# Two layers of attention and feed-forward on one core: a DRAM store, an output transpose and a convolution wait are moved

## The chip, the cores and the metric

The kernel runs on one core of one Trainium2 chip. The metric is the device time of one launch in microseconds (us), the median of three runs. TensorE is PE in the rows (PEld is its weight load), VectorE is DVE, ScalarE is ACT, GpSimd is POOL, and SyncE is SP, which here issues DMAs.

## What is computed

Eight sequences of 512 tokens with 256 features go through two layers. Layer 0 is softmax attention with 16 heads plus a mixture of eight experts. Layer 1, where the change lies, is this (cut to what matters):

```python
def _L1_attn_ref(x, Wqkv_w, Wqkv_b, conv_w, conv_b, out_w, out_b):
    qkv = x @ Wqkv_w.T + Wqkv_b
    q, k, v = ...
    ctx = _causal_attn(q, k, v)
    ctx_c = ctx.reshape(b, s, d).transpose(0, 2, 1)
    conv_out = conv1d(ctx_c, conv_w, padding 1) + conv_b
    q2 = conv_out.transpose(0, 2, 1).reshape(b, s, NUM_HEADS, HEAD_DIM)
    ctx2 = _causal_attn(q2, k, v)
    return ctx2.reshape(b, s, d) @ out_w.T + out_b

xn = _layernorm(x, axis=-1)
x = x + _L1_attn_ref(xn, ...) + _L1_ffn_ref(xn, ...)
```

So each sequence has two causal attentions with the same keys and values: the second one's queries are the first one's output after a convolution over time of width three.

## The kernel before, in words

The kernel is written engine by engine. One class, Engine, holds the plan as generators that yield once per step; each engine's subclass fills in what it does at each step. All engines walk the same plan, so the plan fixes the order of the instructions on each of them, and semaphores (the waits `e.wait_ge`) tie them together. There is no scheduler.

A *unit* is one attention over 8 heads (half of a sequence's 16): `Unit(n, kind, b, c)` with b the sequence and c the half. Kind 0 is layer 0, kind 1 the first attention of layer 1, kind 2 the second. In layer 1 the order is two units of kind 1 (sequence b+1 or so), then two of kind 2 (sequence b), and so on, 32 units numbered 16 to 47. Each unit has two groups g of four heads.

`layer1` interleaves, in each of its rounds, five lanes, one step of each in turn:

- `expp`, the current unit: per step one bank of scores (`scores`, L1111, and the mask L1115), their exponential on ACT (L1959), and some steps later the product with V (`product`, L1128, into the bank PV). After the last product of a group, `close1` runs along with the following steps: `copy_o` (L1969, ACT copies PV to the tile O), `turn_o` (L1138, PE transposes O into bank Mb), `divide` (L1545 and L1553, DVE divides by the row sums and writes the context).
- `maxp`, the next unit: per step one bank of scores for the row maxima (`top`, PE L1072, DVE L1499). After a group, `shift` transposes the maxima (L1094), splits them into three bf16 parts on DVE (L1513 to L1521) and has SP write them as three extra rows of the queries (`rows`: three DMAs t_R<-t_msp of 4 KB). The next unit's scores of that group wait for them.
- `pre1`, the unit after the next: the projection (`part`, L1305 and L1311) for kind 1, or the transposes of the context (`turn_c`, L986) and the convolution (`convolve`, L1331) for kind 2; then the split of queries (z = 0) and keys (z = 1) into three bf16 parts: `high1` on ACT (L1943), `rest` on DVE (the residue t_rr, L1457), `low` on POOL (L2161, L2162), all into the tile spl. `fan1` on SP spreads the parts over the rows of QA or KA by six DMAs of 128 KB each (t_R<-t_spl). For kind 1, `values` on DVE writes V, and on SP it stores the key parts to DRAM (ks<-t_spl, 384 KB), from where the kind 2 unit of the same sequence fans them again (t_R<-ks).
- `fin1`, the unit before: for the second half of a kind 2 sequence the output projection: `turn_f` (L986), `keep_f` (ACT, L2079), `out` (L1354), `add_out`, `store`.
- a short lane in the first round.

Who shares what: bank Mb (`MB[1]`) is used by the query projection of kind 1, by turn_o, turn_c and turn_f; `mbank` waits until the earlier user has been read. The bank PV is free again after copy_o (`pv_read`). The tile cT is read by the convolution, and filled in two halves by ACT (`keep_c`, L2072, semaphore ct_done). All of SP's DMAs share one queue, in program order. On PE the instructions run in order; a wait holds back everything behind it.

Of the kernel before, what the change touches and what calls it, by code (L numbers as in the profile page):

```python
# [63 lines left out]
QK = {}  # L64
# [97 lines left out]
def steps(n):  # L162
    for _ in range(n):
        yield
# [373 lines left out]
class Engine:  # L538
# [216 lines left out]
    def maxp0(self, u):  # L755
        return steps(s1_uses(u))
# [112 lines left out]
    def values(self, u): pass  # L869
    def turn_c(self, u, c): pass  # L870
    def keep_c(self, u, c): pass
    def convolve(self, u, i): pass

    def fin1(self, u):

        if u.kind != 2 or u.c != 1:
            return
        yield from steps(7)
        for c in range(2):
            self.turn_f(u, c)  # L880
            yield
            self.keep_f(u, c)
            yield
        yield from steps(3)
        for h in range(2):
            self.out(u, h)
            yield
            self.add_out(u, h)
            yield
        self.store(u)  # L890
# [50 lines left out]
    def close1(self, u, g):  # L941

        yield
        self.copy_o(u, g)
        yield from steps(3)
        self.turn_o(u, g)
        yield
        self.divide(u, g)
        yield
# [20 lines left out]
class TensorE(Engine):  # L970
# [352 lines left out]
    def convolve(self, u, i):  # L1323
        e, m, s, b, c = self.e, self.m, self.s, u.b, u.c
        if i == 0:
            e.wait_ge(s.d_l2, 80)
            self.mbank(0, s.rr_done, QK[u.n, 0])
            e.wait_ge(s.pads, 1)
        k, cc = i // 2, i % 2
        e.wait_ge(s.ct_done, 2 * b + cc + 1)  # L1330
        t = self.nc.tensor.matmul(m.MB[0][:, :], m.CW[:, i, c * 128:c * 128 + 128], m.cT[:, cc, k:k + 512],  # L1331
                                  start=(i == 0), stop=(i == 5))
        if i == 5:
            t.then_inc(s.qk_mm, 1)
# [941 lines left out]
class SyncE(Engine):  # L2276
# [36 lines left out]
    def fan(self, u, z):  # L2313

        e, m, s = self.e, self.m, self.s
        if u.kind < 2 or z == 0:
            e.wait_ge(s.lo_done, QK[u.n, z])
            to, parts = ((m.QA[u.buf], QP), (m.KA[u.buf], KP))[z]
            of = [m.spl[:, z, p, :] for p in parts]
        else:  # L2320
            e.wait_ge(s.d_ks, 16 * (VN[1, u.b, u.c] - 16))
            to, of = m.KA[u.buf], [m.ks[2 * u.b + u.c][:, p, :].rearrange("(d h) n -> d h n", h=8) for p in KP]
        if u.n in (16, 17):
            e.wait_ge(s.ones_rows, 8)
        elif u.n == 18:
            e.wait_ge(s.y2_mm, 2 * NB)
        elif u.n >= 3:
            e.wait_ge(s.pv_mm, 8 * (u.n - 2))
        for j, part in enumerate(of):
            self.start(to[16 * j:16 * j + 16, :, :], part, s.d_f[z][u.buf])  # L2330

    def maxp0(self, u):
        for g in range(2):
# [57 lines left out]

    def fan1(self, u, z):
        self.fan(u, z)

    def values(self, u):

        self.e.wait_ge(self.s.lo_done, QK[u.n, 1])
        self.start(self.m.ks[2 * u.b + u.c], self.m.spl[:, 1, :, :], self.s.d_ks)

    def store(self, u):  # L2400
        e, m, s, b = self.e, self.m, self.s, u.b
# [101 lines left out]
```

## Time and profile before

| | |
|---|---|
| median of 3 runs | 1987.62 us (1987.46 to 2001.88) |
| profiled execution | 1987.46 us, of which the span from the first to the last instruction is 1985.3 us |
| PE busy | 1798.9 us (91% of the span) |
| DVE busy | 1253.8 us (63%) |
| ACT busy | 1023.6 us (52%) |
| POOL busy | 337.5 us (17%) |
| layer 1 | about 1145 to 1985 us |

Starts are us from the span's start. Busy times of PE overlap in part, since matmuls are pipelined and their ends are modelled. A wait is an engine's idle time with what ended it; idle time of PEld is no loss while PE still works. The distance of 2.16 us between the execution's time and the span lies around the first and last instruction.

### The profile page before, as it was taken

How to read it: one execution, taken by the hardware profiler on the slowest of the kernel's cores; microseconds unless marked ns; L12 is line 12 of the kernel's file. 1: busy time of each engine (PE TensorE's matmuls, PEld its weight loads, DVE VectorE, ACT ScalarE, POOL GpSimd, SP SyncE). 2: the span in 40 equal slices, each digit the busy share in tenths (PEclk: the TensorE clock that was granted, in tenths of full speed). 3: DMA queues.
4: the chain of work that ended last, by engine and by line, in shares of the span. 5: the costliest groups of instructions: out<-in, count | busy, mean ns of one | idle time of the engine just before them, and what ended most of it. 6: DMA issues, size and time to landing. Idle time of an engine off the chain costs nothing.

```text
span 1985.3 us, 31757 instructions
## 1 busy us (share of the span) xinstructions
PE 1798.9 (91%) x10745; PEld 878.4 (44%) x10745; DVE 1253.8 (63%) x3788; ACT 1023.6 (52%) x2064; POOL 337.5 (17%) x525
## 2 busy tenths in 40 slices
PE   4768999999889999998879898999999999999987
PEld 2313555555344454451234343455445454545444
DVE  6675555555654454457563776778787777787673
ACT  1444565555555555554644354555554555555454
POOL 2322211221111221123343200101010101111000
PEclk8878999999999999998999999999999999999999
DMA  6655333434654432441312363645454555455330
GB/s 158 179 143 124 74 68 81 78 76 89 158 125 65 73 59 44 64 57 33 93 33 43 49 83 54 82 74 71 73 72 75 69 84 74 74 84 74 60 50 22
DMA packets 144656, 155.80 MB, mean 78 GB/s; under 512 B 24697, under 2 KB 131473, under 8 KB 144497
## 3 DMA queue, kind: packets, MB, share of 16 engines
q1 hardware_dynamic: 123584, 114.71, 35.4%
q0 software_dynamic: 9024, 14.42, 4.1%
q10 hardware_dynamic: 11888, 24.64, 3.8%
q8 instruction: 87, 1.43, 0.3%
q14 instruction: 73, 0.59, 0.1%
HBM read 55.93 MB, written 33.69 MB: 45 GB/s over the span
## 4 chain that ended last, share of the span: by engine, by line
PE 65%; DVE 12%; DMA 9%; SPq 6%; issue 3%; ACT 2%; POOL 2%; ACTq 0%; DVEq 0%; POOLq 0%
PE p_PV L1128 11%; PE p_S L1111 9%; SPq L2297 6%; PE p_S L1072 5%; PE p_S L1055 5%; PE p_Ma L1331 4%; DMA t_R<-t_msp 4%; PE p_S L1188 4%; PE p_Ma L1211 4%; DVE p_S L1499 3%; PE p_S L1115 2%; DVE t_mx L1485 2%; PE p_Ma L1354 2%; DMA t_xTb<-xTd 1%; PE p_Mb L1211 1%
## 5 line engine op out<-in xcount | busy, mean ns | idle before, releaser
L1959 ACT ACTIVATE t_R<-p_S 128x512 f32<-128x512 f32 (+1 forms) x1216 | 682.7, 578 | 579.9 <-PE p_S L1115 396.1
L1499 DVE CUSTOM_DVE_ANT_0 p_S<-p_S,t_NM 128x128 f32<-128x128 f32 x1008 | 474.6, 514 | 200.3 <-PE p_S L1072 197.2
L1111 PE MATMUL p_S<-t_R 99*128 99x512 bf16 (+3 forms) x1536 | 477.7, 335 | 38.5 <-DMA t_R<-t_msp 17.0
L1485 DVE TENSOR_REDUCE t_mx<-p_S 128x1 f32<-128x512 f32 x512 | 347.0, 686 | 252.6 <-PE p_S L1055 250.5
L1128 PE MATMUL p_PV<-t_R 128*17 128x512 f32 (+3 forms) x3072 | 331.8, 504 | 1.3 <-ACT t_R L1959 1.0
L1072 PE MATMUL p_S<-t_R 96*128 96x128 bf16 x1008 | 254.5, 304 | 19.3 <-DMA t_R<-t_spl 10.2
L1111 PEld LDWEIGHTS p_S<-t_R 99*128 99x128 bf16 x1536 | 151.1, 99 | 179.0 <-ACT t_R L1959 69.0
L1055 PE MATMUL p_S<-t_R 96*128 96x512 bf16 x512 | 203.0, 399 | 27.0 <-DVE t_mx L1485 16.9
L1115 PE MATMUL p_S<-t_NM 128*128 128x128 bf16 x1024 | 199.2, 220 | 0.0
L2161 POOL CAST t_spl<-t_rr 128x512 bf16<-128x512 f32 x80 | 49.2, 615 | 866.8 <-DVE t_rr L1457 866.8
L1499 DVE DVE_READ_ACCUMULATOR2_ANT t_mx<- 128x1 f32 x1024 | 143.5, 140 | 0.1
L1072 PEld LDWEIGHTS p_S<-t_R 96*128 96x128 bf16 x1008 | 80.9, 98 | 139.6 <-DVE t_mx L1499 53.8
L1115 PEld LDWEIGHTS p_S<-t_NM 128*128 128x128 bf16 x1024 | 101.2, 99 | 68.7 <-issue 44.0
L1055 PEld LDWEIGHTS p_S<-t_R 96*128 96x128 bf16 x512 | 50.2, 99 | 168.7 <-issue 84.6
L1188 PE MATMUL p_S<-t_R,t_NM 128*128 x184 | 96.3, 605 | 6.8 <-DMA t_NM<-hTd 6.4
L1128 PEld LDWEIGHTS p_PV<-t_R 128*17 128x17 f32 x3072 | 51.1, 95 | 115.5 <-issue 112.9
L1331 PE MATMUL p_Ma<-t_NM,t_R 128*128 128x512 f32 x192 | 99.0, 612 | 0.1
L1211 PE MATMUL p_Ma<-t_R,t_NM 128*128 x360 | 94.6, 385 | 0.0
L2162 POOL TENSOR_TENSOR t_spl<-t_rr,t_spl 128x512 bf16<-128x512 f32 x80 | 93.2, 1164 | 6.5
L1211 PEld LDWEIGHTS p_Ma<-t_R,t_NM 128*128 128x128 f32 x360 | 68.2, 192 | 24.8 <-issue 10.2
L2046 ACT ACTIVATE t_R<-p_S,t_R 128x512 f32<-128x512 f32 x64 | 43.5, 687 | 61.3 <-PE p_S L1260 59.5
L2220 POOL DMA_DIRECT2D ysd<-t_NM x39 | 34.0, 871 | 215.1 <-ACT t_NM L2014 215.1
(282 smaller groups left out, 2153.7 us busy)
## 6 DMA issues: line engine op xcount, KB each, us to landing
t_R<-t_spl SPq DMA_DIRECT2D x480, 128.0 KB
t_R<-in_w ACTq DMA_DIRECT2D x32, 512.0 KB, 6.9
t_R<-ks SPq DMA_DIRECT2D x96, 128.0 KB
ks<-t_spl SPq DMA_DIRECT2D x16, 384.0 KB, 5.1
hTd<-t_NM SPq DMA_DIRECT2D x39, 128.0 KB, 2.6
ysd<-t_NM SPq DMA_DIRECT2D x39, 128.0 KB
t_NM<-hTd SPq DMA_DIRECT2D x39, 128.0 KB, 2.3
ysd<-t_NM POOLq DMA_DIRECT2D x39, 128.0 KB, 3.1
```

What stands on the lines that cost most here:

```text
L1055: self.nc.tensor.matmul(m.S1[s1_bank(k)][:, :], qa[0:96, 4 * g + j, qb * 128:(qb + 1) * 128], ka[0:96, 4 * g + j, 0:512], start=True, stop ...
L1072: t = self.nc.tensor.matmul(bank[:, z, :], qa[0:96, h, qb * 128:(qb + 1) * 128], ka[0:96, h, 0:n], start=True, stop=True)
L1111: t = self.nc.tensor.matmul(bank[:, z, :], ka[0:99, h, kb * 128:(kb + 1) * 128], qa[0:99, h, n0:512], start=True, stop=not u.causal)
L1115: t = self.nc.tensor.matmul(bank[:, z, 0:128], m.identb, m.maskk, start=False, stop=True)
L1128: t = self.nc.tensor.matmul(m.PV[32 * j:32 * j + 17, n0:512], vt[:, kb, 4 * g + j, :], m.P1[kb][j] if u.causal else m.P[p % 2][:, j, :], s ...
L1188: z = self.nc.tensor.matmul(m.MB[i][:, :], m.hT[t % 2][:, c, :], m.W1[:, bass.ds(self.regs[t], 1), c, :], start=(c == 0), stop=(c == 1))
L1211: x = self.nc.tensor.matmul(M[:, 0:256], m.AT[:, k, :], m.W2[:, bass.ds(self.regs[t], 1), k * 256:k * 256 + 256], start=(k == 0), stop=(p ...
L1331: t = self.nc.tensor.matmul(m.MB[0][:, :], m.CW[:, i, c * 128:c * 128 + 128], m.cT[:, cc, k:k + 512], start=(i == 0), stop=(i == 5))
L1485: nc.vector.tensor_reduce(m.mx[:, g, 4 * j + qb:4 * j + qb + 1], m.S1[s1_bank(k)][:, :], AX.X, ALU.max).then_inc(s.s1_read, 1)
L1499: x = nc.vector.tensor_tensor_reduce(out=sc, in0=sc, in1=m.maskq[:, 512 - n:512], scale=1.0, scalar=NEG, op0=ALU.add, op1=ALU.max, accum_o ...
L1959: nc.scalar.activation(m.P1X[kb][j0 // per] if u.causal else m.P[p % 2][:, j0:j0 + per, :], m.s2_bank(k)[:, 0:per * n].rearrange("p (j n) ...
L2297: self.raw.dma_start(to, of).then_inc(sem, 16)
```

## The change

Four edits, all of layer 1.

1. The store of the key parts (ks<-t_spl), which SP issued in `values` at the end of a kind 1 unit's pre1 lane, is issued in `fan`, directly behind the fan of the keys (z = 1). The wait in front of it goes, as the fan has already waited for the same semaphore. Kind 1 units 16 and 17 had nothing between the two.
2. `close1` has one step less between copy_o and turn_o, so turn_o and divide come one step earlier on PE and DVE, in all 64 groups.
3. `fin1` takes one step from before turn_f and gives it to the pause behind keep_f: turn_f and keep_f come one step earlier, out stays where it was.
4. `convolve` waits for both halves of cT before its first matmul instead of for each half before the first matmul that reads it.

```diff
@@ fin1
-        yield from steps(7)
+        yield from steps(6)
         for c in range(2):
             self.turn_f(u, c)
             yield
             self.keep_f(u, c)
             yield
-        yield from steps(3)
+        yield from steps(4)
@@ close1
         self.copy_o(u, g)
-        yield from steps(3)
+        yield
+        yield
         self.turn_o(u, g)
         yield
         self.divide(u, g)
@@ TensorE.convolve
         if i == 0:
             e.wait_ge(s.d_l2, 80)
             self.mbank(0, s.rr_done, QK[u.n, 0])
+            e.wait_ge(s.ct_done, 2 * b + 2)
             e.wait_ge(s.pads, 1)
         k, cc = i // 2, i % 2
-        e.wait_ge(s.ct_done, 2 * b + cc + 1)
@@ SyncE.fan
         for j, part in enumerate(of):
             self.start(to[16 * j:16 * j + 16, :, :], part, s.d_f[z][u.buf])
+        if u.kind == 1 and z == 1:
+            self.start(m.ks[2 * u.b + u.c], m.spl[:, 1, :, :], s.d_ks)
@@ SyncE
-    def values(self, u):
-
-        self.e.wait_ge(self.s.lo_done, QK[u.n, 1])
-        self.start(self.m.ks[2 * u.b + u.c], self.m.spl[:, 1, :, :], self.s.d_ks)
```

In the changed kernel turn_o and all lines behind it are numbered one higher (L1138 is L1139), those behind the edit of fan three higher, and those behind the removed `values` two lower.

On PE, at the end of a unit's second group while a kind 1 unit is being projected, these rows stand before (L1138 is turn_o, p_Mb the bank that the query projection also uses, L1072 the maxima matmul, L1128 the product):

```order
L1111 MATMUL p_S<-t_R 128x384 [waits s2_exp]
L1115 MATMUL p_S<-t_NM 128x128
L1072 MATMUL p_S<-t_R 128x512 [waits s1_read]
L1111 MATMUL p_S<-t_R 128x384 [waits s2_exp]
L1115 MATMUL p_S<-t_NM 128x128
L1128 MATMUL p_PV<-t_R 17x512 [waits pv_read]
L1128 MATMUL p_PV<-t_R 17x512 x3
L1138 MATMUL p_Mb<-t_ident,t_O 128x128 [waits rr_done]
L1138 MATMUL p_Mb<-t_ident,t_O 128x128 x3
L1072 MATMUL p_S<-t_R 128x384 [waits s1_read]
```

and these after:

```order
L1112 MATMUL p_S<-t_R 128x384 [waits s2_exp]
L1116 MATMUL p_S<-t_NM 128x128
L1139 MATMUL p_Mb<-t_ident,t_O 128x128 [waits pv_read,rr_done]
L1139 MATMUL p_Mb<-t_ident,t_O 128x128 x3
L1073 MATMUL p_S<-t_R 128x512 [waits s1_read]
L1112 MATMUL p_S<-t_R 128x384 [waits s2_exp]
L1116 MATMUL p_S<-t_NM 128x128
L1129 MATMUL p_PV<-t_R 17x512 x4
L1073 MATMUL p_S<-t_R 128x384 [waits s1_read]
```

The four transposes moved ahead of one maxima matmul, one bank of scores and the product; the waits for the copy of PV (pv_read) and for the residue of the queries (rr_done) moved with them.

On SP, in such a unit, before (t_spl to t_R is the fan, t_msp to t_R the rows of maxima, ks the store):

```order
L2297 DMA t_R<-t_spl 16x8x512 [waits lo_done]
L2297 DMA t_R<-t_spl 16x8x512 x5
L2297 DMA t_R<-t_msp 1x16x128 [waits msp_done]
L2297 DMA t_R<-t_msp 1x16x128 x2
L2297 DMA ks<-t_spl 128x1536
```

and after:

```order
L2298 DMA t_R<-t_spl 16x8x512 [waits lo_done]
L2298 DMA t_R<-t_spl 16x8x512 x5
L2298 DMA ks<-t_spl 128x1536
L2298 DMA t_R<-t_msp 1x16x128 [waits msp_done]
L2298 DMA t_R<-t_msp 1x16x128 x2
```

The store passed three small DMAs and their wait. This happens in 14 units.

## Rows read from the trace of the kernel before

**Rows 1.** Time windows: length, busy of each engine (instructions), granted PE clock, DMA share, GB/s.

```profile
1300.00:1400.00 100.00, 96.50 (x762) 50.27 (x761) 78.24 (x311) 54.76 (x104) 10.60 (x12) 1.00 0.53 76
...
1200.00:1900.00 700.00, 667.35 (x5137) 342.44 (x5135) 522.29 (x2063) 366.02 (x698) 68.89 (x78) 0.99 0.50 73
```

**Rows 2.** Waits, 1125 to 1985: who waited for whom: us in total, times, longest.

```profile
DVE p_S L1499 <- PE p_S L1072: 194.7, 235, 5.8
...
PE p_S L1111 <- DMA t_R<-t_msp: 17.0, 15, 2.1
...
PEld p_Mb L1138 <- DVE t_rr L1457: 11.1, 13, 0.9
PE p_S L1072 <- DMA t_R<-t_spl: 10.2, 2, 5.1
...
PEld p_Ma L1331 <- ACT t_NM L2072: 5.1, 6, 0.8
...
PE p_Ma L986 <- DVE t_R L1553: 1.9, 2, 0.9
```

**Rows 3.** Chain that ended last, one unit boundary: start, us, what.

```profile
1362.35 0.29 DVE t_msp L1521
...
1363.24 0.59 SPq L2297
...
1363.88 5.32 DMA t_R<-t_msp
```

**Rows 4.** Timeline of SP's queue at the same boundary: start, us, what.

```profile
1353.91 8.56 SPq L2297 DMA_DIRECT2D t_R<-t_spl  x12
1362.65 1.81 SPq L2297 DMA_DIRECT2D t_R<-t_msp  x3
1364.51 0.58 SPq L2297 DMA_DIRECT2D ks<-t_spl  x1
```

**Rows 5.** DMA issues, 1364 to 1372 (last: us to landing); then t_msp in layer 1.

```profile
ks<-t_spl SPq DMA_DIRECT2D x1, 384.0 KB, 5.1
...
DMA to landing us min/median/max: 1.6/2.2/6.5
```

**Rows 6.** Time windows at that boundary, columns as in rows 1.

```profile
1357.00:1366.00 9.00, 8.99 (x80) 5.39 (x80) 7.87 (x35) 5.17 (x10) 0.00 (x0) 1.00 1.14 127
...
1367.50:1368.00 0.50, 0.50 (x10) 0.49 (x8) 0.50 (x3) 0.00 (x0) 0.00 (x0) 1.00 0.95 335
```

**Rows 7.** Timeline of PE: first scores of two units; in brackets idle before, releaser.

```profile
1578.43 0.39 PE L1111 MATMUL p_S<-t_R 99*128 99x512 bf16 x1 [2.09 <-DMA t_R<-t_msp]
1604.74 0.39 PE L1111 MATMUL p_S<-t_R 99*128 99x512 bf16 x1 [0.77 <-DMA t_R<-t_msp]
```

**Rows 8.** Timeline, 1346.5 to 1354.5, a closing with a kind 1 projection.

```profile
1349.22 0.58 ACT L1969 COPY t_O<-p_PV 128x512 f32<-128x512 f32 x1
...
1351.19 0.22 PE L1115 MATMUL p_S<-t_NM 128*128 128x128 bf16 x1
...
1351.23 0.73 DVE L1457 SCALAR_TENSOR_TENSOR t_rr<-p_Mb,t_BQK,t_spl 128x512 f32<-128x512 f32 x1
...
1351.78 1.05 PE L1128 MATMUL p_PV<-t_R 128*17 128x512 f32 x8
...
1352.76 0.66 PE L1138 MATMUL p_Mb<-t_ident,t_O 128*128 128x128 f32 x4
...
1353.62 0.57 DVE L1499 CUSTOM_DVE_ANT_0 p_S<-p_S,t_NM 128x384 f32<-128x384 f32 x1 [0.99 <-PE p_S L1072]
```

**Rows 9.** Timeline of PE: first and last of twelve such waits.

```profile
1200.41 0.39 PE L1072 MATMUL p_S<-t_R 96*128 96x512 bf16 x1 [0.20 <-DVE t_mx L1499]
...
1929.44 0.39 PE L1072 MATMUL p_S<-t_R 96*128 96x512 bf16 x1 [0.20 <-DVE t_mx L1499]
```

**Rows 10.** Chain that ended last, start of a convolution.

```profile
1293.90 0.86 PE p_Ma L1331 x2
...
1294.78 1.12 PE p_Ma L1331 x2
```

## The prediction

> **What bounds the kernel now.** I read the profile in this order: the time windows, the waits by total, the chain that ended last, and the timeline around four places. Every edit lies in layer 1, the last 840 us of the span, so the first two layers keep their time.
>
> The windows [rows 1] show TensorE busy 667.35 of 700 us from 1200 to 1900, and 96.50 of 100 in an ordinary stretch, at full granted clock. TensorE (PE) sets the pace, and about 3 us in 100 are left. The waits [rows 2] say what ends those: 15 waits for the row-maximum rows (t_R<-t_msp, 17.0 us together), two for the fan of query parts (10.2 us), and little else. A weight-load row (PEld) is no stall by itself: it may wait while PE still streams. ACT and DVE wait for PE far more than PE for them: DVE's maxima alone sat idle 194.7 us.
>
> In the chain [rows 3] one unit boundary reads: DVE ends the split maxima at 1362.64, SP issues three small DMAs, the third leaves at 1363.88, lands 5.32 us later, and PE goes on. In SP's timeline [rows 4] the same three stand behind twelve fan DMAs of 128 KB, and the store to ks follows them. The shortest landing of t_msp in layer 1 is 1.6 us, the median 2.2 [rows 5]; 5.3 means that it waited behind other bytes. The windows agree [rows 6]: the DMA engines are full from 1357 to 1368, at 127 GB/s for the fan and 335 GB/s at its end, where the store runs. So at the start of these units PE waits for the DMA backlog, by 0.77 us at the lesser and 2.09 at the most [rows 7].
>
> **The change part by part.** The sum is made against the profiled execution, 1987.46 us (span 1985.3 and 2.16 around it); the median of the three runs is 1987.62, the same thing.
>
> *The store to ks, before the rows of maxima.* 14 units of kind 1 (all but the first two) have it in front now. Its issue takes 0.58 us [rows 4]. It cannot make the rows land earlier, since it stood behind them, so a gain is excluded. It can make them later. In the trace the store was issued at 1364.51 and landed 5.1 us later, at 1369.61; the third row DMA landed at 1363.88 + 5.32 = 1369.20 [rows 3, 5]. The queue holds the same bytes in either order, so what now stands last should land when the last one did: 0.4 us later, 14 x 0.4 = 5.6 us, all on the path since PE waits there. The far end: the rows wait for the whole store. 384 KB at the 335 GB/s of [rows 6] is 1.2 us, 14 x 1.2 = 16.8 us (at the fan's 127 GB/s it would be 3.1 us each, 43 us, but the store's own stretch is nearer). The near end is 0. I take 0.4 because it is read from the two landings themselves.
>
> The Trainium skill (DMA: Bandwidth & Descriptors, section on queues, rings and completion order) speaks against this edit: a semaphore increment is a strongly ordered write, which lands only after every earlier write of the same DMA engine. By that rule the small rows cannot be reported before the store ahead of them; the trace's two landings make that 0.4 us each, 5.6 in all, and the trace has no case of rows behind a store.
>
> *Turning the output (turn_o, L1138) one step earlier.* PE executes the same four transposes, 64 times, before the next maxima matmul instead of behind the PV product. That work only moves; what counts is what it now waits for. (a) The copy of PV to O: at 1349.22 + 0.58 = 1349.80 it is long done when PE comes to the new place, at 1351.19 + 0.06 (the chain's price of that matmul) = 1351.25 [rows 8]. I cost it at nothing; ACT's copy sits ahead of two further exponentials, and that hides it. (b) Bank Mb: in 13 units of kind 1 it is still read by the residue of the query (L1457, DVE), from 1351.23 to 1351.96 [rows 8]. Before, PE was still busy with the PV product, from 1351.78 until turn_o at 1352.76, when that was over; the 13 PEld waits of 0.9 us for t_rr [rows 2] are its shadow. Now PE stands 0.7 us, and behind it the maxima matmul, so DVE too: 13 x 0.7 = 9.1 us if it counts. But this stall comes after the residue that starts the fan, and the fan's backlog ends this unit: PE then waited at least 0.77 us for it [rows 7]. So the stall eats that wait, and I take 0, with 9.1 as the other end. (c) At 12 closings PE idled 0.20 us before the maxima matmul, waiting for DVE [rows 9]; the transposes now fill that gap: -12 x 0.2 = -2.4 us (ends: 0 where a later wait takes it back, and -4). (d) The division follows one step earlier on DVE. At the first and last batch the conv's transpose (L986) waited for it, 1.9 us in two waits [rows 2]; both go, and what is late next is the transpose's own turn on PE: -1.9 us (ends 0 and -1.9), as the chain from there to the 5.1 us fan wait is serial.
>
> *The convolution's wait.* The first of six matmul groups now waits for both halves of cT. In the chain [rows 10] it ran 0.86 us from 1293.90 and the second began at 1294.78, when ACT's copy was just done: it filled exactly the wait. Six waits of that kind stand in [rows 2]. Now PE stands idle for it: 6 x 0.86 = 5.2 us. Behind it are the scores that ACT lives from, and the rest of that chain is PE. In the two outer batches six spare steps lie between, so nothing. Ends: 0 and 5.2.
>
> *turn_f and keep_f one step earlier, output step unchanged.* Same instructions, one exponential ahead of the other on ACT; its divide moved by as much. 0.
>
> Sum: 5.6 + 0 + 5.2 - 2.4 - 1.9 = +6.5 us, so 1994.0 us, 0.3% over. A measurement of this kernel tells from no change about 1%, some 20 us.
>
> **The rivals.**
> 1. *The residue stall is not absorbed.* If the landing follows from when the rows are issued, not from the backlog, all of DVE and SP shift by 0.7 us and the 9.1 us show: 2003.1. For it: the 5.3 us are counted from the issue. Against it: full DMA engines until 1368 [rows 6].
> 2. *The rows wait out the whole store* (slower). Place: the first scores of 14 units. Price: 16.8 instead of 5.6, 2005.2; with the first rival 2014.3. Above 1.4 us each (25.3 us in all, for 19.9 us net) it passes 1%. For it: the store's bytes are moved at the very end of the backlog, where nothing runs beside them; against it: the two landings are 0.4 apart.
> 3. *The waits for the rows go* (faster). DVE starved 0.99 us before one maxima reduction because PV and turn_o stood together ahead of its matmul [rows 8]. If splitting them brings DVE forward, maxima are split earlier and the 17.0 us of waits vanish: 1987.5 - 17.0 + 5.2 - 2.4 - 1.9 = 1971.4. Against it: the backlog, not the maxima, ends those waits, and the bytes stay.
> 4. *The edits cancel or miss*, with the conv wait hidden by a later wait and the store free: 1987.5 - 4.3 = 1983.2, to 1987.5.
>
> **How the numbers follow.** Forecast 0.58 (own range 1989 to 2000), rival 1 0.12, rival 2 0.12, rival 3 0.08, rival 4 0.10. The range 1983 to 2009 holds the forecast, rival 4, rival 1 and the lower half of rival 2, and leaves out some 0.15. Slower by over 1% (above 2007.5) is the upper half of rival 2 and its sum with rival 1: 0.11. Faster by over 1% (below 1967.6) is more than rival 3 gives: 0.03. Within 1%: 0.86.
>
> **What would show it.** In the profile after: the store's issue directly behind the fan; the waits of PE for t_msp grow or stay (17 us becoming 12 to 23, since the stall takes 0.7 of each and the store gives 0.4); a new PE wait for t_rr of about 0.7 us, 13 times; a new PE wait for ACT's cT copy of 0.9 us, six times; the 0.20 us waits before the maxima matmuls gone; the conv's transpose without its two waits of 0.9. The distance from a fan's first issue to the next unit's first score (1353.91 to 1369.24, 15.3 us) should become 15.7. I am wrong if that distance grows by a microsecond or more (rival 2), if it grows by 0.7 although the store is cheap (rival 1), or if it shrinks (rival 3).

## The result and the profile after

The changed kernel takes 2016.25 us (median of 4 runs, 2015.55 to 2017.11) beside 1990.63 us for the kernel before on the same chip (4 runs): ratio 1.0118, 95% interval 1.0077 to 1.0162. The forecast was 1994.0 us in a range of 1983 to 2009. The direction was right; the size, +6.5 us, was not. The profiled execution took 2013.77 us (span 2011.5), 26.3 us more than the one before.

Windows of the kernel after, columns as in [rows 1]:

```profile
1300.00:1400.00 100.00, 94.75 (x747) 48.62 (x746) 75.23 (x292) 52.47 (x99) 10.62 (x12) 1.00 0.53 78
1200.00:1900.00 700.00, 653.86 (x4983) 334.46 (x4983) 511.79 (x2008) 356.83 (x675) 67.21 (x76) 0.98 0.49 71
```

Beside [rows 1], PE is 13.5 us less busy in the same 700 us, and its mean granted clock is 0.98 instead of 0.99. So time went in two ways: PE waits more, and it runs slower for a while. The two executions differ before layer 1 too: unit 16's first score, up to which both do the same work, comes at 1125.60 us before and at 1123.24 after, and in the traces of the other runs at 1121.7 to 1134.6. A difference of some us between two whole executions therefore means little, and below I compare stretches of layer 1. The waits from 1125 on, to be read against [rows 2]:

```profile
DVE p_S L1500 <- PE p_S L1073: 214.1, 205, 5.4
...
PE p_S L1112 <- DMA t_R<-t_msp: 24.0, 17, 2.3
...
PE p_S L1073 <- DMA t_R<-t_spl: 9.4, 2, 4.7
PE p_Mb L1139 <- DVE t_rr L1458: 8.0, 13, 0.6
...
PE p_Ma L1332 <- ACT t_NM L2073: 5.8, 6, 1.0
...
PE p_Mb L987 <- ACT t_xTb L2080: 3.5, 8, 0.7
```

The waits for the rows of maxima grew from 17.0 to 24.0 us. Three waits are new on PE: turn_o behind the residue, the convolution for cT (no longer in PEld's shadow), and turn_f for the copy of its first half.

The queue of SP at the unit boundary of [rows 4]:

```profile
1355.76 9.21 SPq L2298 DMA_DIRECT2D t_R<-t_spl  x12
1365.01 0.60 SPq L2298 DMA_DIRECT2D ks<-t_spl  x1
1365.65 1.82 SPq L2298 DMA_DIRECT2D t_R<-t_msp  x3
```

The chain that ended last, at the same place, with the first score behind it (compare [rows 3]):

```profile
1366.88 4.86 DMA t_R<-t_msp
1371.75 0.05 issue
1371.79 0.39 PE p_S L1112
```

From the fan's first issue to the next unit's first score it is now 16.03 us instead of 15.33. Over the 12 boundaries of this kind behind unit 20's first score, the mean is 16.61 us (15.95 to 17.27) instead of 15.61 (15.20 to 16.52): +1.0 us each, where 0.4 was forecast. This takes in what the other edits do; the store's own part comes below.

For what follows I cut the stretch from unit 18's first score to unit 47's into its 29 intervals between first scores of units. They are grouped by what is projected meanwhile, since the store, the fan and the convolution hang on that. The last group is everything else (second halves of kind 2, the two outer batches). The stretch runs from 1178.63 to 1950.78 before, and from 1179.06 to 1976.15 after.

| us | 12 with a kind 1 projection | 6 with a convolution | 11 others | stretch |
|---|---|---|---|---|
| before | 303.40 | 175.46 | 293.29 | 772.15 |
| after | 315.40 | 192.39 | 289.30 | 797.09 |
| of it lost to the clock, before | 1.7 | 0 | 8.5 | 10.2 |
| of it lost to the clock, after | 1.7 | 8.5 | 5.1 | 15.4 |

So +12.0, +16.9 and -4.0 us, 24.9 of the 26.3. The time lost to the clock is 1 minus the granted clock, added up over the stretch; what that means is shown below. Of the -4.0 us, 3.4 are fewer such losses and no merit of the change. The six intervals with a convolution are 29.24 or 29.25 us long in the kernel before, and 32.27 to 32.34 in five of six after, 30.79 in the sixth. That is two amounts, about 1.5 us each. One is no wait: a window over such an interval after, with 0.95 as its mean granted clock (the last three columns are clock, DMA share and GB/s):

```profile
1507.81:1540.15 32.34, 30.82 (x214) 17.17 (x215) 19.68 (x76) 14.56 (x29) 1.77 (x2) 0.95 0.39 58
```

and over the same interval before:

```profile
1498.28:1527.52 29.24, 29.09 (x214) 16.19 (x215) 19.62 (x77) 14.47 (x29) 1.77 (x2) 1.00 0.43 64
```

The same 214 matmuls keep PE busy 1.7 us longer. Cut into windows of 1 us, the kernel after shows where:

```profile
1508.00:1509.00 1.00, 1.00 (x15) 0.39 (x14) 0.00 (x0) 0.60 (x1) 0.00 (x0) 0.99 0.00 0
1509.00:1510.00 1.00, 1.00 (x8) 0.93 (x6) 0.78 (x7) 0.00 (x0) 0.00 (x0) 0.50 0.00 0
1510.00:1511.00 1.00, 1.00 (x11) 0.15 (x8) 0.33 (x4) 0.39 (x1) 0.00 (x0) 0.50 0.00 0
1511.00:1512.00 1.00, 1.00 (x9) 0.87 (x6) 0.28 (x1) 0.69 (x2) 0.00 (x0) 0.50 0.00 0
1512.00:1513.00 1.00, 1.00 (x9) 0.77 (x8) 0.59 (x4) 0.16 (x1) 0.00 (x0) 0.80 0.00 0
```

The granted clock falls from 1.00 to 0.50, that is from 2.4 to 1.2 GHz, just behind the unit's first score, and PE is fully busy at half speed. Adding 1 minus the clock over these windows gives 1.7 us lost. What PE did before stands in its timeline; the first scores of four units:

```profile
1398.28 0.39 PE L1112 MATMUL p_S<-t_R 99*128 99x512 bf16 x1 [1.99 <-DMA t_R<-t_msp]
...
1481.77 0.39 PE L1112 MATMUL p_S<-t_R 99*128 99x512 bf16 x1 [1.59 <-DMA t_R<-t_msp]
...
1507.81 0.39 PE L1112 MATMUL p_S<-t_R 99*128 99x512 bf16 x1 [1.54 <-DMA t_R<-t_msp]
...
1591.69 0.39 PE L1112 MATMUL p_S<-t_R 99*128 99x512 bf16 x1 [2.31 <-DMA t_R<-t_msp]
```

Between 1230 and 1890 the clock falls six times after (behind waits of 1.96, 1.99, 1.54, 1.65, 1.64 and 2.16 us) and once before (at 1579, behind the wait of 2.09 us of [rows 7]). Each costs about 1.7 us. It does not fall behind 1481.77 or 1591.69, so the length of the wait alone does not decide. Five of the six follow at the start of an interval with a convolution. The clock also falls outside these bounds, more often before than after: over the whole stretch it cost 10.2 us before and 15.4 after, so the change's part is 5.1 us. Taking these losses out, the stretch grew by 19.8 us. That is an estimate, as PE need not be what everything waits for in each of them: the convolution intervals show 1.56 us for each 1.71.

### The profile page after: what moved, and what is told of

The parts are those of the page before. It is cut to its first block, busy times and chain, and to the rows that moved or that the text cites. A ratio compares the mean times of both kernels' runs of the same rounds, so it can differ in the third digit from the quotient of the medians.

```text
span 2011.5 us, 31811 instructions
## 1 busy us (share of the span) xinstructions
PE 1807.4 (90%) x10745; PEld 880.9 (44%) x10745; DVE 1258.2 (63%) x3788; ACT 1025.9 (51%) x2064; POOL 337.4 (17%) x525
## 4 chain that ended last, share of the span: by engine, by line
PE 61%; DVE 14%; DMA 10%; SPq 6%; issue 4%; ACT 3%; POOL 2%; ACTq 0%; DVEq 0%; POOLq 0%
PE p_PV L1129 11%; PE p_S L1112 8%; SPq L2298 6%; DMA t_R<-t_msp 5%; PE p_S L1056 5%; PE p_Ma L1332 4%; PE p_S L1073 4%; PE p_S L1189 4%; PE p_Ma L1212 4%; DVE p_S L1500 3%; PE p_Ma L1355 2%; DVE t_mx L1486 2%; PE p_S L1116 1%; DMA t_xTb<-xTd 1%; PE p_S L1212 1%
## 5 line engine op out<-in xcount | busy, mean ns | idle before, releaser
L1056 PE MATMUL p_S<-t_R 96*128 96x512 bf16 x512 | 203.2, 399 | 26.6 <-DVE t_mx L1486 16.8
L1212 PEld LDWEIGHTS p_Ma<-t_R,t_NM 128*128 128x128 f32 x360 | 68.3, 192 | 24.7 <-issue 10.2
```

Source lines behind the costliest of these rows:

```text
L1056: self.nc.tensor.matmul(m.S1[s1_bank(k)][:, :], qa[0:96, 4 * g + j, qb * 128:(qb + 1) * 128], ka[0:96, 4 * g + j, 0:512], start=True, stop ...
L1212: x = self.nc.tensor.matmul(M[:, 0:256], m.AT[:, k, :], m.W2[:, bass.ds(self.regs[t], 1), k * 256:k * 256 + 256], start=(k == 0), stop=(p ...
```

## The experiments

Every ratio is to the kernel before, run on the same chip. Line numbers in rows are each kernel's own.

### Each edit alone

The store alone, as in edit 1:

```diff
@@ SyncE.fan
+        if u.kind == 1 and z == 1:
+            self.start(m.ks[2 * u.b + u.c], m.spl[:, 1, :, :], s.d_ks)
```

> The kernel before with only the store to ks moved behind the fan. Theory S (the store ahead of the rows is most of the loss): 14 boundaries at which the rows land about 1.0 us later, 14 us, and longer PE waits behind which the granted clock falls to 0.50 more often, 3 to 8 us: 2001 to 2010 us in all, PE waits for t_msp 28 us or more instead of 17.0, more dips of the clock than the one (at 1579) in the ordinary stretches of before. Theory T (the loss is the stall of turn_o behind t_rr, which delays the rows): the store costs what its landing said, 0.4 each, 5.6 us: about 1993 us, waits for t_msp 22 us, and no more dips.

Ratio 1.0114 (1.0077 to 1.0152), +22.7 us. The wait of its PE:

```profile
PE p_S L1111 <- DMA t_R<-t_msp: 27.6, 16, 2.9
```

17.0 became 27.6 us, and its timeline has nine falls of the clock between 1230 and 1890 where before has one. The store alone is as slow as the whole change. But in the stretch of this trace (797.32 us, +25.2) the clock lost 27.2 us, 16.9 more than before, and what is left is +8.2: the waits are the smaller part here, and the falls that they bring on the larger. Over all executions of this kernel, 1 minus the mean clock times the span is 92.7 us on average (4), and 79.3 for the kernel before (25). The distance from fan to next first score is 16.41 us (12 boundaries), +0.80.

The output transposes one step earlier (edit 2), alone:

```diff
@@ close1
-        yield from steps(3)
+        yield
+        yield
```

> The kernel before with only turn_o and divide one step earlier. Theory S: 13 stalls of 0.6 us behind t_rr appear, but the waits for t_msp fall by as much (17 to about 9 us), so the time is the same or up to 4 us lower (1983 to 1988 us). Theory T: the stalls show: 1993 to 1997 us, waits for t_msp stay at 17 us or more.

Ratio 0.9977 (0.9955 to 0.9998), -4.6 us. Its waits:

```profile
PE p_S L1112 <- DMA t_R<-t_msp: 12.8, 17, 1.6
...
PE p_Mb L1139 <- DVE t_rr L1458: 8.0, 13, 0.6
```

The stall behind the residue is there, 13 x 0.6 us, and the kernel is not slower for it. The distance from unit start to fan start stays 9.54 us, and the waits for the rows fall by 4.2 us: a good part is absorbed, as the prediction had it. Not all is: the 12 intervals with a kind 1 projection take 1.6 us more (304.98 instead of 303.39), with the same loss to the clock, and the six with a convolution 0.10 us each. In the stretch (770.18 us, -2.0) the clock lost 3.4 us less than before; without that it is +1.4. The same holds over all executions: the clock lost 72.1 us on average here (10) and 79.3 before (25), and the rest is 2.8 us more, with an uncertainty of 3. So the faster ratio is the clock's; whether the edit brought fewer falls or chance did is not shown.

The convolution's wait (edit 4) and turn_f with keep_f (edit 3), each alone:

```diff
@@ TensorE.convolve
+            e.wait_ge(s.ct_done, 2 * b + 2)
...
-        e.wait_ge(s.ct_done, 2 * b + cc + 1)
```

> The kernel before with only the convolution's first matmul waiting for both halves. Both theories: six waits of 0.9 us, +5.2 us, 1993 us; if a later wait swallows them 1987.5 us. Should the wait also bring the granted clock down, more.

```diff
@@ fin1
-        yield from steps(7)
+        yield from steps(6)
...
-        yield from steps(3)
+        yield from steps(4)
```

> The kernel before with only turn_f and keep_f one step earlier. By the prediction nothing: 1987.5 us. By the waits of the changed kernel (eight waits of 0.4 us of turn_f for ACT's copy, 3.5 us together): 1991 us.

Measured, in this order: 1.0029 (1.0005 to 1.0052), +5.8 us, and 1.0016 (0.9997 to 1.0035), +3.2 us, which by itself is not told from none. The traces decide it: the interval with a convolution takes 30.16 us in all six cases with edit 4 alone and 29.76 with edit 3 alone, so +0.92 and +0.52 us. The stretches take 776.46 and 774.50 us, each with 8.5 lost to the clock: +6.0 and +4.1 beside the kernel before, without the clock's losses. The row of edit 3:

```profile
1309.61 0.66 PE L986 MATMUL p_Mb<-t_ident,t_NM 128*128 128x128 f32 x4 [0.41 <-ACT t_xTb L2079]
```

turn_f's second half uses bank Mb again and waits for the copy of the first, which ACT has queued behind an exponential. The four ratios add up to +27 us, and the change as a whole cost 26, but that is a chance match: the store alone lost 16.9 us more to the clock, the whole change 5.1. Without the clock's losses the four stretches are +8.2, +1.4, +6.0 and +4.1, together 19.8 us, and the changed kernel's is +19.8.

### Everything but the store, and a third of the store

Edits 2, 3 and 4, with the store left where it was:

> The changed kernel with the store put back behind the rows. If the single edits add up (turn_o -4.6, convolution +5.8, turn_f +3.2 us in their own runs): +4.4 us over before. If the store and the stalls only cost together: +10 us or more.

Ratio 1.0045 (1.0028 to 1.0062), +8.9 us. Its intervals: 303.84, 184.71, 290.78, together 779.33 us. Without the clock's losses that is +10.6, so the store adds 9.2 us to the other three edits. The distance from fan to next first score is 15.77 us (12 boundaries), and the changed kernel's is 0.84 above it. The convolution intervals are 30.78 or 30.79 us, all six, at full clock. So of the +3.1 us that they have in the changed kernel, 1.54 belong to edits 4, 3 and 2 (0.92, 0.52 and 0.10) and 1.56 to the clock.

With one of the store's three parts ahead of the rows and two behind them:

```diff
@@ SyncE.fan
+        if u.kind == 1 and z == 1:
+            self.start(m.ks[2 * u.b + u.c][:, 0, :], m.spl[:, 1, 0, :], s.d_ks)
@@ SyncE.values
+        self.start(self.m.ks[2 * u.b + u.c][:, 1:3, :], self.m.spl[:, 1, 1:3, :], self.s.d_ks)
```

> The kernel before with one third of the store (128 KB) ahead of the rows and two thirds behind them; one more DMA issue per unit. Theory bytes (the rows wait until the store's bytes have passed): a third of the moved store's price, PE waits for t_msp 20 to 21 us (17.0 before, 27.6 with all of it ahead), time +5 to +10 us. Theory receipt (any write to DRAM ahead of the rows delays their report by its own receipt, whatever its size): the waits near 27 us, time +18 us or more.

Ratio 1.0069 (1.0041 to 1.0096), +13.7 us.

```profile
PE p_S L1111 <- DMA t_R<-t_msp: 20.6, 15, 2.2
```

The waits are as the theory of bytes had them: 17.0, 20.6 and 27.6 us with 0, 128 and 384 KB ahead. The mean distance from fan to next first score, over the same 12 boundaries, is 15.61, 15.90 and 16.41 us. That is about 0.3 us for each 128 KB; at the 335 GB/s of [rows 6] 128 KB take 0.39 us. A fixed price for one write to DRAM ahead, the other theory, would have been the same for both. The total is above what the theory gave, since the clock falls more often here too: of the stretch's +12.8 us (784.90), 10.2 are lost to it and 2.5 are not, a third of the whole store's 8.2.

### The rows from another queue

The three row DMAs of layer 1 issued by ACT, everything else as before:

```diff
@@ ScalarE (SyncE.rows returns at once for causal units)
+        for x in range(3):
+            self.raw.dma_start(m.QA[u.buf][96 + x:97 + x, 4 * g:4 * g + 4, :], m.msp[:, x, :]).then_inc(s.d_mq[u.buf][g], 16)
```

> The kernel before with the three row DMAs of layer 1 issued by ACT, so that they do not stand behind the fan in SP's queue. Theory backlog (5.3 us to landing is place in SP's queue): they land within about 3 us, PE's 17.0 us of waits for t_msp go, 10 to 20 us faster unless ACT, now blocked by the wait for msp_done and by three issues per group, stops the exponentials. Rival (the DMA engines are full whatever the queue): landing stays at 5 us, and the time stays or rises.

Ratio 1.0123 (1.0105 to 1.0142), slower. The DMA issues of this kernel, 1130 to 1990 (the last column is the median from issue to landing), and its waits:

```profile
t_R<-t_msp ACTq DMA_DIRECT2D x189, 4.0 KB, 3.8
```

```profile
ACT t_R L1959 <- issue: 100.0, 39, 4.0
...
PE p_S L1111 <- ACT t_R L1959: 29.7, 58, 2.2
```

The rows land no sooner: the median is 3.8 instead of the 2.2 us of [rows 5], and PE still waits 12.5 us for them. One thing blurs this: SP no longer waits for the maxima, so at 11 of the 14 boundaries its store is issued ahead of ACT's first row. At the three others it comes behind the first row and ahead of the third. So the run does not tell the fan's bytes from the store's; it shows that rows from a second issuing queue did not go round the bytes of the first. And ACT, which waits for the maxima and then issues, is idle in front of its exponentials 39 times for no reason that the profile shows.

### What the clock's part is

The store moved, and five matmuls of 512 columns ahead of the wait at all 31 unit starts, so that PE is not idle there:

> The kernel with only the store moved, plus five matmuls of 512 columns at each unit's start, ahead of the wait for the rows, whose result the real scores overwrite (added work, output unchanged). Theory clock (about half of the 22.7 us is time at the granted clock of 0.50 behind waits of about 2 us): PE idles 1.1 us less per boundary, the dips behind the rows' waits go, and the time falls by 5 to 12 us, though 5 x 31 matmuls are added. Rival (the waits alone are the price): no faster, slower by the matmuls at the boundaries without a wait, 16 x 1 us.

Ratio 1.0120 (1.0098 to 1.0141). The clock no longer falls in the ordinary stretch, yet the total was no lower than with the store alone. That did not settle it: the fillers cost about 1.1 us at each of the 17 starts that have no such wait (the six convolution intervals are 30.32 us, 1.08 above 29.24). Over all executions this adds up: the clock lost 70.4 us on average here and 92.7 with the store alone, 22 less, and the rest of the span is 19 us longer, where 17 x 1.08 is 18.4. So they were put only where PE waits anyway, into the changed kernel:

```diff
@@ TensorE.scores
+        if 17 <= u.n < 47 and (UNITS0 + UNITS1)[u.n + 1].kind == 1 and g == kb == j0 == 0:
+            for _ in range(FILLERS):
+                self.nc.tensor.matmul(m.s2_bank(k)[:, :], ka[0:96, 0, 0:128], qa[0:96, 0, 0:512], start=True, stop=True)
```

> Added work: the changed kernel, with five score-like matmuls of 512 columns, which nobody reads, in front of the wait for the rows of maxima, at the 14 unit starts alone whose fan is that of a kind 1 unit (about 1.1 us of TensorE work; those starts wait 1.08 to 2.3 us anyway). Theory (a part of the loss is the clock): the granted clock of 0.50 behind these starts goes, and with it 8 x 1.7 = 14 us, so about 2002 us or 12 over before, with t_msp waits down from 24 to about 10 us. Rival (what e8_store_fill seemed to say: the clock gives nothing back): the dips go but the time stays at 2013 or more. Of e8 I say that the 17 fillers at starts without a wait cost 1.1 us each, which hid the gain; this run tells.

Ratio 1.0072 (1.0042 to 1.0101) where the changed kernel had 1.0118: by the two ratios 9 us back; by the stretch of the traces 7.2 us (789.87 instead of 797.09). That a kernel with more work is faster is what the clock's theory asked for, though the gain is less than the 14 expected; the two intervals overlap, so the traces carry it. In the stretch the clock lost 6.8 us instead of 15.4, 8.5 less; over all executions it is 73.0 us (5) against 82.1 in the changed kernel (5), 9 less. The window over the same interval as above, in this kernel:

```profile
1517.47:1548.25 30.78, 29.27 (x215) 16.21 (x216) 19.69 (x77) 14.58 (x29) 1.77 (x2) 1.00 0.38 61
```

All six such intervals are 30.78 or 30.79 us at full clock, as in the kernel without the store's move. The waits for the rows are 10.8 us, and with 14 x 1.08 us of filler that is 25.9 instead of 24.0: the filler overshoots some waits, which may be a part of the miss. Besides, the expectation counted eight falls, and in the stretch six went (10.2 us) while one near its end became 1.7 us dearer.

### Does the landing follow the fan's start?

If the rows land when the backlog ends, then an earlier fan should bring them forward one for one. The residue of the queries moved one step earlier on DVE, with edit 2 and alone:

```diff
@@ pre1
             self.high1(u, 0)
             if u.n >= 18:
                 self.part(u, 1, 0)
+                self.rest(u, 0)
             yield
-            self.rest(u, 0)
```

> Before, with turn_o one step earlier (as in e2_turn) and the residue of the queries (DVE t_rr, z = 0) in the step of its ACT rounding instead of one later. Theory (the landing of the rows hangs on when the fan starts): the residue runs about 0.4 us earlier in 14 units, SP's fan starts as much earlier, the t_msp waits fall from e2_turn's 12.8 to about 7 us and the new t_rr stall from 8.0 to about 3; total 4 to 6 us under e2_turn, that is about 9 under before (ratio 0.995). Rival: the residue now stands ahead of one maxima reduction on DVE, which delays PE's next maxima matmul by up to 0.7 us each: total as e2_turn or above it.

> Before, with only the residue of the queries one step earlier on DVE. Theory: the fan starts 0.4 us earlier, t_msp waits 17.0 falls to about 11 to 12 us, total -5 us (ratio 0.9975). Rival: the maxima reduction behind the residue comes 0.7 us late on DVE and the gain is eaten: ratio 1.000 or above.

Together: 1979.82 us, ratio 0.9936 (0.9910 to 0.9962). Alone: 0.9981 (0.9963 to 0.9999). In both the fan starts 9.07 us behind the unit's start instead of 9.54, and the distance from fan to next first score stays 15.70 and 15.68 us (before 15.61). The waits of the first:

```profile
PE p_S L1113 <- DMA t_R<-t_msp: 10.3, 15, 1.6
```

So the landing follows the fan's start: without the clock's losses the 12 intervals with a kind 1 projection shorten by 4.9 us in the second kernel, 0.41 each for the 0.47. The expected 7 us of waits were 10.3; as both ends of the wait moved forward, most of the gain shows in shorter units and not in shorter waits. The version with both edits is faster than both kernels of this case, by 0.6% over the one before.

Then a further step, with both halves of the query projection in one step of PE:

```diff
@@ pre1
             self.part(u, 0, 0)
-            yield
+            if u.n < 18:
+                yield
             self.part(u, 0, 1)
```

> e10_turn_rest, and both halves of the query projection of a kind 1 unit in one step on TensorE (from unit 18 on), so that everything behind it in that lane, the fan too, comes one step earlier (a step of that place is about 1.8 us, two together with the residue). Theory (the rows land when the backlog ends, and the backlog ends as much earlier as the fan starts earlier): the fan starts 1.5 us or more earlier at 14 boundaries, the t_msp waits fall from 10.3 to under 4 us, the t_rr stall in front of turn_o goes; about 6 to 8 us under e10_turn_rest, ratio 0.990 to before. Rival 1: something else is late then (the keys' fan, or POOL's casts), so that the waits go by half only: ratio 0.992 to 0.994. Rival 2: the doubled projection on TensorE holds back the exponentials at the start of each of these units, whose scores are short: ratio above 0.995.

Ratio 0.9978 (0.9960 to 0.9997), worse than the step before it. The fan typically starts 9.77 us behind the unit's start, where the other kernels have 9.54 or 9.07. SP's queue in this kernel:

```profile
1352.99 1.77 SPq L2300 DMA_DIRECT2D t_R<-t_msp  x3
1354.86 2.55 SPq L2300 DMA_DIRECT2D t_R<-t_spl  x4
```

POOL had the query's parts ready at 1352.57, but the rows of the other group stand ahead of the fan in the queue, and they had to wait for DVE. DVE and POOL in the same place:

```profile
1351.91 0.74 DVE L1522 CAST t_msp<-t_mrr 16x128 bf16<-16x128 f32 x1
```

```profile
1351.41 1.16 POOL L2165 TENSOR_TENSOR t_spl<-t_rr,t_spl 128x512 bf16<-128x512 f32 x1
```

The cast of maxima takes 0.21 us elsewhere; beside POOL's subtraction it takes 0.73 and ends 0.08 us behind it, in all 13 cases of layer 1 (the other 50 casts take 0.21). The waits for the rows were 16.3 us, not half of 10.3, and the ratio lies where rival 2 had it. But the 12 intervals with a kind 1 projection are 0.75 us longer each than in the step before, without the clock's losses, and the fan starts 0.70 later: that covers nearly all of it, and leaves little for rival 2's late exponentials. So something else was late, as rival 1 has it, and it was the queue of SP.

## Why the prediction missed

No single term carries the miss. In the stretch the clock is 5.1 us that stood nowhere, turn_o is 5.7 us over its forecast, turn_f and keep_f 4.1, the store 3.4 (8.2 beside 12 x 0.4) and the convolution 0.8.

**The store: the term 14 x 0.4 was mis-sized.** The step that failed reads: "The queue holds the same bytes in either order, so what now stands last should land when the last one did". It holds for the bytes and not for the landing of the rows. At the boundary shown, the store landed 15.70 us behind the fan's start before (1369.61) and 15.45 after (issued at 1365.01, landed 6.2 later); the rows landed 15.98 behind it, at 1371.74. In windows of 0.5 us of the kernel after:

```profile
1370.00:1370.50 0.50, 0.50 (x10) 0.38 (x7) 0.50 (x3) 0.00 (x0) 0.00 (x0) 1.00 0.24 82
1370.50:1371.00 0.50, 0.21 (x1) 0.00 (x0) 0.44 (x3) 0.47 (x1) 0.00 (x0) 1.00 0.05 15
1371.00:1371.50 0.50, 0.00 (x0) 0.00 (x0) 0.50 (x2) 0.13 (x1) 0.00 (x0) 1.00 0.00 0
1371.50:1372.00 0.50, 0.21 (x1) 0.11 (x2) 0.01 (x1) 0.00 (x0) 0.00 (x0) 1.00 0.00 0
```

The queue is empty from 1371.0 on, and PE gets its signal at 1371.75. The measured term is 0.80 us for each boundary with the store alone, and 0.84 on top of the other edits: 14 x 0.8 = 11.2 us, twice the forecast and two thirds of rival 2's 16.8. By the stretches, which hold 12 of the 14, it is 8.2 to 9.2 us. So the rows wait for most of the store's bytes, and rival 2 was nearer than the forecast. Its test stood in the text ("wrong if that distance grows by a microsecond or more"), and the distance grew by 1.0, of which the stall of turn_o is a part. I had preferred two landings 0.4 apart, which told in what order things finish and not what the rows pay behind the store. The rows' own last packet ends 0.9 us before they are reported at this boundary, in both kernels alike; so that gap did not grow with the store ahead, and what came later is the moving of the rows' bytes. The Trainium skill (DMA: Bandwidth & Descriptors, section Anatomy of one DMA — SWDGE (gpsimd) path) says of DMAs issued by GpSimd that the completion waits until the last byte is confirmed in the target memory, and that HBM is the slowest target. These DMAs are issued by SP; a gap between last byte and report is there, but no run here moves a store to another target, and what the gap is made of stays open.

**The clock: a term that was missing.** The prediction said "at full granted clock" of an ordinary stretch and went on with waits alone. A longer wait at a unit's start now and then costs 1.7 us more, at 1.2 GHz, than the wait itself. The trace before had one such case in its ordinary stretch, behind the wait of 2.09 us that stood in [rows 7]; I read the wait and did not look at the clock behind it. Six falls instead of one between 1230 and 1890 are 5 x 1.7 = 8.5 us, and the filler run gave back 7 to 9. Over the whole stretch it is 5.1, as the kernel before lost 3.4 more at its two ends. With the store alone it was 16.9. So the size of this term varies. What is shown is that the longer waits bring more falls: between 1230 and 1890 the traces have 9, 6 and 6 in the three kernels with all or a third of the store ahead of the rows and no filler, none in the two with fillers, and 0 to 2 in the nine others. The Trainium skill (TensorE: Matmul & The Clock Gate, section HAM oscillation) describes this pattern, a wait for a DMA and then matmuls at the lower clock each time; the traces agree that it recurs, though not each time: they show it behind waits as short as 1.54 us and not behind one of 2.31. What decides between them is open.

**turn_f and keep_f: forecast 0, measured +0.52 us in each of the intervals with a convolution (3.1), and 4.1 in the stretch without the clock's losses.** The step was "one exponential ahead of the other on ACT". It looked at ACT's order and not at bank Mb, which turn_f's two halves share.

**The convolution: forecast 6 x 0.86 = 5.2, measured 6 x 0.92 = 5.5 by its intervals** (5.8 us by ratio). Right.

**turn_o: forecast -4.3, measured +1.4 in the stretch without the clock's losses.** The ratio's -4.6 us matches the forecast by luck, since that kernel lost 7 us less to the clock in its executions. The reason was right in part. The stall was absorbed but for some 0.13 us at each boundary, and rival 1 (9.1 us in full) falls, since the fan starts at 9.54 us in both kernels and the waits for the rows shrank by 4.2 where 8.0 of new stall came in. As forecast, the twelve waits of 0.20 us and the two of the conv's transpose are gone. But the twelve all lay in the 11 other intervals, where two new ones of 0.42 and 0.49 us came in, and these intervals are only 0.7 us shorter without the clock's losses. What took the rest is not shown.

By what was measured in the stretch: 8.2 + 1.4 + 6.0 + 4.1 = 19.8 us (with unrounded terms) and 5.1 for the clock are 24.9, beside the stretch's 24.9. Each term is from one execution, and the ratios have intervals of about +-4 us, so a part of this match is luck too. The forecast for the same terms was 5.6 - 4.3 + 5.2 + 0, and nothing for the clock. One sum of the prediction does not come out: a store that takes the total 19.9 us up costs 19.0 us (14 x 1.4), not 25.3.

The chance given to "slower by over 1%" was 0.11. Rival 2 alone would not have reached it; what did was the other terms and the clock on top. The range was too narrow because its bounds were set term by term, and no bound was set for what a longer wait does to the engine that waits.

## What to carry to other kernels

A small DMA that an engine waits for belongs ahead of every large one in its queue: each 128 KB ahead of it instead of behind it cost 0.3 us here. To bring such a landing forward, start the backlog earlier or shrink it, and check what else stands in the queue in front (of 0.47 us of an earlier fan 0.41 came through; one more step made the fan later). When a change lengthens waits of the engine that sets the pace, look at the granted clock right behind the longest waits of that kind in the trace before, and put a price on more of them. And before a small gain or loss is put down to an edit, take out what each execution lost to the clock: here a gain of 4.6 us was not left as a gain.

## What the runs showed of the hardware beyond that

A wait of PE of 1.5 to 2.2 us can be followed by some us at 0.50 of the clock that cost 1.7 us each time, and five matmuls that nobody reads, in each such wait, took 7 us off the stretch. An issuing engine is not free: three DMAs of 4 KB took 1.8 us of SP's or ACT's queue, and with them on ACT the idle time in front of its exponentials that nothing else explains was 100 us in all. DVE's cast of 16x128 from SBUF to SBUF went from 0.21 to 0.73 us where it met POOL's subtraction, 13 times of 13, and ended 0.08 us behind it; by the Trainium skill (SBUF — State Buffer, section SBUF: two separate sides) the two share a port pair under an exclusive lock, and these rows agree.
